# Causal attention: the mask of the exponentials as a selection on GpSimd, the maxima split there, the outputs copied by ScalarE

## The reference

```python
q = qkv[:, :, :, :Q_PER_KV].reshape(B, S, N_HEADS, HEAD_DIM)   # S = 1024, 32 heads of 16, 4 per kv head
k = qkv[:, :, :, Q_PER_KV]
v = qkv[:, :, :, Q_PER_KV + 1]
...
scores = jnp.einsum('bqhd,bkhd->bhqk', q, k) * SM_SCALE
scores = jnp.where(mask[None, None], scores, jnp.finfo(scores.dtype).min)
probs = jax.nn.softmax(scores, axis=-1)
ctx = jnp.einsum('bhqk,bkhd->bqhd', probs, v).reshape(B, S, HIDDEN)
```

## Time and profile before

| what | value |
|---|---|
| median of 3 runs | 1382.53 us (1381.4 to 1382.91) |
| the profiled execution | 1387.69 us |
| its span | 1385.9 us |
| mean granted TensorE clock | 0.904 |
| PE busy | 1159.6 us (84%) |
| DVE busy | 862.5 us (62%) |
| ACT busy | 661.4 us (48%) |
| POOL busy | 479.0 us (35%) |

### The profile page before, as it was taken

The page is one execution under the profiler, slowest core; times in us unless marked ns, Lnnn a source line. Parts: engine busy times, 40 slices in busy tenths (PEclk is TensorE's granted clock), DMA queues, the critical chain, the costliest instruction groups (busy, mean ns, idle before and its releaser), DMA issues. The chain is left out here.

```text
span 1385.9 us, 22738 instructions
## 1 busy us (share of the span) xinstructions
PE 1159.6 (84%) x6056; PEld 737.9 (53%) x6057; DVE 862.5 (62%) x1624; ACT 661.4 (48%) x1202; POOL 479.0 (35%) x434
## 2 busy tenths in 40 slices
PE   5979999995294999999997796999999908777687
PEld 4746766763172344444434574667766605455454
DVE  4857777772465888788852656777777524445542
ACT  3136666663232366666674121666666503324133
POOL 4325555553772111111113224455555442050030
PEclk9979999998597699999998897999999957978879
DMA  9256898556314430000001363779955550000001
GB/s 355 88 214 142 242 244 230 107 103 117 141 56 119 104 69 2 1 1 1 1 1 38 127 231 131 214 193 262 257 111 99 83 164 1 15 24 0 12 20 61
DMA packets 63497, 151.71 MB, mean 109 GB/s; under 512 B 12560, under 2 KB 17488, under 8 KB 58832
## 3 DMA queue, kind: packets, MB, share of 16 engines
q1 hardware_dynamic: 40224, 99.83, 21.0%
q0 software_dynamic: 22592, 50.27, 18.5%
q10 hardware_dynamic: 624, 0.92, 0.4%
HBM read 105.81 MB, written 44.97 MB: 109 GB/s over the span
## 5 line engine op out<-in xcount | busy, mean ns | idle before, releaser
L715 POOL DMA_INDIRECT moe_acc_rows<-moe_out_rows,moe_token_of x94 | 165.4, 1760 | 198.2 <-ACT moe_out_rows L790 194.9
L1721 DVE TENSOR_REDUCE causal_top<-causal_mx 128x1 f32<-128x512 f32 (+3 forms) x384 | 192.4, 551 | 52.2 <-PE causal_mx L1588 44.7
L1694 ACT ACTIVATE causal_prob<-causal_sc 128x512 f32<-128x512 f32 (+3 forms) x384 | 171.7, 489 | 94.1 <-PE causal_sc L1611 73.7
L819 DVE TENSOR_TENSOR moe_w_lo<-moe_raw,moe_w_hi 128x1024 fp32r<-128x1024 f32 x94 | 115.2, 1225 | 112.5 <-ACT moe_w_hi L778 100.5
L730 PE MATMUL moe_gu<-moe_raw,moe_xt_plain 128*128 x376 | 180.5, 603 | 2.3 <-ACT moe_w_hi L778 2.3
L1585 PE MATMUL causal_mx<-causal_ks,causal_qs 96*128 (+4 forms) x384 | 131.6, 349 | 28.0 <-DMA causal_qs<-causal_parts 15.6
L778 ACT CAST moe_w_hi<-moe_raw 128x1024 fp32r x94 | 98.2, 1045 | 94.4 <-issue 86.5
L1607 PE MATMUL causal_sc<-causal_qs,causal_ks 99*128 (+3 forms) x384 | 125.3, 334 | 1.3 <-ACT causal_prob L1694 1.0
L708 POOL DMA_INDIRECT moe_rows<-moe_xn_rows,moe_token_of x94 | 93.0, 990 | 75.9 <-DVE moe_z L828 31.5
L822 DVE TENSOR_TENSOR moe_down_lo<-moe_raw,moe_down_hi 128x1024 fp32r<-128x1024 f32 x94 | 114.5, 1219 | 0.0
L735 PE MATMUL moe_gu<-moe_w_hi,xt_hi 128*128 128x512 f32 x188 | 112.7, 599 | 0.0
(11 more groups left out here) (275 smaller groups left out, 2459.3 us busy)
## 6 DMA issues: line engine op xcount, KB each, us to landing
moe_raw<-in_w_gu SPq DMA_DIRECT2D x34, 1024.0 KB
moe_raw<-in_w_down SPq DMA_DIRECT2D x34, 512.0 KB
causal_qs<-causal_parts SPq DMA_DIRECT2D x42, 128.0 KB, 3.3
moe_acc_rows<-moe_zeros SPq DMA_DIRECT2D x2, 2304.0 KB, 15.2
moe_acc_rows<-x SPq DMA_DIRECT2D x18, 256.0 KB, 2.0
moe_xn_rows<-xn SPq DMA_DIRECT2D x2, 2048.0 KB, 10.7
x<-moe_acc_rows SPq DMA_DIRECT2D x16, 256.0 KB, 5.2
xn<-moe_acc_rows SPq DMA_DIRECT2D x16, 256.0 KB, 5.6
```

What stands on the lines that cost most here:

```text
L715: pool.indirect_dma_start(acc_rows[a], bass.IndirectOffsetOnAxis(ap=token_of[:, b - 3:b - 2].bitcast(U32), axis=0), out_rows[(b - 3) % OUT ...
L819: nc.vector.tensor_tensor(w_lo[1 - s][:, :, :], raw[:, bass.ds(at + SPLIT_AT, GU_COLS - SPLIT_AT)].rearrange("p (k n) -> p k n", k=SPLIT), ...
L1694: nc.scalar.activation(prob[u % 2][:, h, o:CH], sc[(u * QPK + h) % BANKS][:, o:CH], ACT.Exp, scale=SCALE).then_inc(exp_done, 1)
L1721: nc.vector.tensor_reduce(top[:, kc, t, h:h + 1], mx[i % BANKS][:, 0:w], AX.X, ALU.max).then_inc(mx_read, 1)
```

## The change

Five things change together, all inside this block.

1. The mask product of the exponentials (L1611) is gone, and with it the tile `mask_kq`. POOL instead sets the masked probabilities of a diagonal block to zero after ACT has written them, by one selection over four heads of 128 columns (`mask`), and the value products of these steps wait for it.
2. `split_maxima` is moved from DVE to POOL. DVE keeps the maximum over both key halves (`later_best`).
3. `read_output` is moved from DVE to ACT.
4. The turn of the second half's maxima moves from the end of step 0 to the end of step 1, with the reading of them in step 2, and the turn of the last outputs from step 1 to step 2, the division behind it from step 2 to step 3.
5. POOL's list is written out for all groups and has no loop.

```diff
 @block.gpsimd
+def split_maxima(gn, h):
+    if h:
+        pool.wait_ge(best_done, gn + 1)
+        source = best[:, :, :]
+    else:
+        pool.wait_ge(mx_read, gn * NMU + HALF0)
+        source = top[:, 0, 0:TC, :]
+    nc.gpsimd.tensor_scalar(neg[:, :, :], source, -1.0, None, ALU.mult).then_inc(neg_chain, 1)
+    ...
+def mask(g, u):
+    c, kb = STEPS[u]
+    o = kb * P - c * CH
+    pool.wait_ge(exp_done, g * (NS * QPK) + ((u + 1) * QPK + BANKS))
+    nc.gpsimd.affine_select(prob[u % 2][:, :, o:o + P], prob[u % 2][:, :, o:o + P], [[0, QPK], [1, P]],
+                            ALU.is_ge, 0.0, base=0, channel_multiplier=-1).then_inc(masked, 1)
+def group(g, first, more):
+    if not first:
+        split_maxima(g, 1)
+    values(g)
+    for u in range(NS):
+        if u in DIAGONAL:
+            mask(g, u)
+        if u == 1 and not first:
+            put_maxima(g, 1)
+        if u == C0 - 1 and more:
+            split_maxima(g + 1, 0)
+        if u == C0 + 2 and more:
+            put_maxima(g + 1, 0)
 @block.tensor
 def scores(g, u, h):
-    nc_last = nc.tensor.matmul(sc[b][:, o:CH], ..., start=True, stop=not diagonal)
-    if diagonal:
-        nc_last = nc.tensor.matmul(sc[b][:, o:o + P], ident[:, :], mask_kq[:, :], start=False, stop=True)
-    nc_last.then_inc(sc_done, 1)
+    nc.tensor.matmul(sc[b][:, o:CH], ..., start=True, stop=True).then_inc(sc_done, 1)
 def values(g, u):
-    pe.wait_ge(exp_done, g * (NS * QPK) + ((u + 1) * QPK + BANKS))
+    if u in DIAGONAL:
+        pe.wait_ge(masked, g * len(DIAGONAL) + (DIAGONAL.index(u) + 1))
+    else:
+        pe.wait_ge(exp_done, g * (NS * QPK) + ((u + 1) * QPK + BANKS))
 def group(g, first, more):
-    if u == 0 and not first:
+    if u == 1 and not first:
         pe.wait_ge(ctx_done, g * NCH)
         turn_maxima(g, 1)
-    if u == 1 and not first:
+    if u == 2 and not first:
         pe.wait_ge(neg_read, g * NCH + 2)
         turn_output(g - 1, 1)
 @block.scalar
+def read_output(g, c):
+    act.wait_ge(pv_done, g * NS + ((C0, NS)[c] + 1))
+    act.wait_ge(out_turn, g * NCH + (c + 1))
+    nc.scalar.copy(out_t[:, :], po[:, :]).then_inc(po_read, 1)
 def group(g, first, more):
-    if u == 1 and h == 0 and not first:
+    if u == 2 and h == 0 and not first:
         read_maxima(g, 1)
+    if u == 0 and not first:
+        read_output(g - 1, 1)
+    if u == C0:
+        read_output(g, 0)
 @block.vector
-def split_maxima(gn, h, units):
-def read_output(g, c):
+def later_best(gn):
+    dve.wait_ge(mx_read, gn * NMU + NMU)
+    nc.vector.tensor_tensor(best[:, :, :], top[:, 0, TC:T, :], top[:, 1, TC:T, :], ALU.max).then_inc(best_done, 1)
 def group(g, first, more):
-    if u == 2 and not first:
+    if u == 3 and not first:
         normalise(g - 1, 1)
```

More of the change, by code:

```diff
@@ L1485, in causal_attention_layer @@
             v_now = sb("v_now", [P, T, 2 * HD])
-            masks = sb("masks", [P, 2, P])
+            later = sb("later", [P, P])
             mask_qk = sb("mask_qk", [P, P], BF16)
-            mask_kq = sb("mask_kq", [P, P], BF16)
             ident = sb("ident", [P, P], BF16)
@@ L1768, in group @@
                             if more:
-                                for i in range(UPS - 1):
+                                for i in range(UPS):
                                     maximum(g + 1, UPS * u + i)
-                            if u == 0 and not first:
-                                read_output(g - 1, 1)
-                            if u == 2 and not first:
+                            if u == 3 and not first:
                                 normalise(g - 1, 1)
-                            if u == C0:
-                                read_output(g, 0)
-                            if more:
-                                maximum(g + 1, UPS * u + UPS - 1)
-                                if UPS * (u + 1) == HALF0:
-                                    split_maxima(g + 1, 0, HALF0)
                             if u == C0 + 5:
@@ L1987, in layout @@
     later = np.where(np.arange(P)[None, :] > np.arange(P)[:, None], np.float32(-1e30), np.float32(0))
-    d["masks"] = f(np.stack([later, later.T], axis=1).astype(np.float32))
+    d["later"] = f(later)
     return d
```

96 lines of the change are left out of this document (43 added, 53 removed).

## The result

The changed kernel takes **1369.76 us** (median of 4 runs, 1367.37 to 1373.52); before takes 1382.72 in the runs beside it. The ratio is **0.9909, 95% interval 0.989 to 0.9928**. A second series of the same kernel gave 1367.03 against 1380.55 (ratio 0.9908, 0.9891 to 0.9924). The forecast was 1390, slower; the change makes the kernel 13 us faster. The time lies in the range on record, the sign is wrong.

A forecast was written before the change was run, and what follows sets the result against it. PE's list was taken to bound the block. Seven middle groups at 34.95 us against 35.24 gave -2.0 us, the last group +7.7, the start +1.4: +7.1 in total, a median of about 1390 us, range 1368 to 1409.

The forecast's parts named there:

- What is A?: POOL's selection of 512 elements in diagonal steps: A, its time, taken as 1.05 us, ends 0.40 and 1.69.
- The slope of the sum: Whole kernel: total change 64A - 60.1 us, so +7.1 us at A = 1.05.
- as quick as the cast or quicker: Rival on POOL's selection: A = 0.84 gives -6 us, 1376; A = 0.40 gives about 1359; chance 0.35.
- The hand-offs: Diagonal steps, either side of POOL's selection: 0.25 us from ACT to POOL, 0.10 from POOL to PE.
- the break-even: Selection time at which the forecast's summed change for the whole kernel is zero: A = 0.94 us.
- the formula on record: Whole kernel: 64A - 60.1 us; a middle group takes 26.55 + 8A us against 35.24.
- spare time: Diagonal steps: how long A may be before PE stalls, 0.12 to 0.81 us, together 4.95 a group.
- PE's own gaps: Gaps before the value products of twelve steps, without waits for masks: 21.7 us a group.
- Beyond 0.81 each diagonal step adds all of A: Eight diagonal steps of a group: above that selection time, PE's stalls are 8A - 4.95 us.
- The stalls at u = 0 and 4 are worth about 1.3 us each: PE's waits for DVE before value products of steps 0 and 4: go when split and output copy leave DVE.
- The price of 0.06 for a mask product: Mask products on PE: 0.06 us each, 32 in a group, so 1.8 us saved.
- The step 0 selection comes 0.45 us late by this, on the path.: Group start on POOL: split (1.65 us) and value copy (0.40) precede step 0's selection, adding 0.45 us a group.

The follow-up runs named there:

- both edits: Changed kernel with the mask product on PE in the last group and the first-half output turn and division a step earlier: 1364.92 us, ratio 0.9877; repeated 1365.64 us.

## Why the prediction was wrong

**"What is A?" is the step that failed.** It took 1.05 us, "the middle between the cast and the two-input operation, since the predicate is generated and not read". Measured is 0.64, below the cast, though not below the end of 0.40. The slope of the sum at that place is what made it fatal: 64 selections by 0.41 us are 26 us, against a forecast of +7.1. The error in reasoning is to take the predicate as an addition to a pass over the data. The rows said less than I read from them: the comparison that "takes twice the cast" differs from it by its kind of operand and its output format as well, so its extra time was never shown to be the predicate's. The rival "as quick as the cast or quicker", with 0.35, was the right case; its own figure for the cast (1376) was above the result because even the cast is slower.

Here the Trainium skill was nearer than the choice made against it. GPSIMD Engine Reference, Performance versus the Vector engine, gives 768 ns for 512 elements in a tight loop without data-dependent branching, as a best case; that this is the price of a one-input operation is the prediction's reading. This trace shows less still, 640 ns for that many elements with a predicate on top; where they differ the measurement decides, and that figure is no lower bound for this instruction.

**The hand-offs were too dear.** "I take 0.25, and 0.10 from POOL to PE": the first was read from the earlier trace rows, in which POOL issues a DMA behind ACT's copy. For a compute instruction the same way costs 0.06. That is 0.24 us too much in each diagonal step, and it is a part of what set the break-even at 0.94 where 1.03 was measured. By that straight line even the forecast's own 1.05 would have given no change and not a slower kernel. With the right A the formula on record gives 64 x 0.64 - 60.1 = -19.1 us for a block that gained 15.0. It fits no better because it also counts a spare time larger than A as a gain: at A = 0.64 the steps 1, 2, 3, 5 and 9 have 0.55 us of it too much in each group, 3.85 us in seven groups. -15.3 is left. So three errors stand side by side. The hand-offs make the stalls 0.44 too large in a group (0.72 for the 0.28 that remain). PE's own gaps were taken too short: 21.7 and 0.45 for step 0, 22.15 together, where 22.9 was measured with the remaining stalls in it. These two cancel nearly; the price does not.

**"Beyond 0.81 each diagonal step adds all of A"**: this form is right only far out. From 0.64 to 0.98 a group grew by 1.0 us where eight steps grew by 2.7, from 0.98 to 1.22 by 1.1 where they grew by 1.9. With the true hand-offs the spare times are 0.36 (step 0) to 1.05, so at 0.64 only step 0 stalls, and at 0.98 still not all do.

**The savings.** "The stalls at u = 0 and 4 are worth about 1.3 us each": 3.32 to 2.06 and 3.00 to 2.09, so 1.26 and 0.91. The run without the selection gives them free of the mask products, which the forecast counted apart: 3.32 to 1.97 and 3.00 to 2.26, so 1.35, of which 0.3 was the turn that moved on, and 0.74. Both stalls were taken too large. The reason for DVE's relief holds: without the splits' move nothing is gained. Of the two, the splits are worth four times the outputs, each put back alone. The price of 0.06 for a mask product was right where PE is the bound; 32 of them are 1.9 us and not the 1.8 written, and 0.92 of it arrives. (Step 2's gap, 1.86 in the forecast's list, should be 1.81 by its own rule.)

**"The step 0 selection comes 0.45 us late by this, on the path."** POOL's timeline at a group's start shows the queue:

```profile
563.47 0.25 POOL L1558 TENSOR_SCALAR causal_neg<-causal_best 128x16 f32<-128x16 f32 x1 [0.29 <-DVE causal_best L1786]
563.79 0.20 POOL L1563 CAST causal_neg_parts<-causal_neg 128x16 bf16<-128x16 f32 x1
...
564.64 0.22 POOL L1572 TENSOR_TENSOR causal_neg_parts<-causal_left,causal_neg_parts 128x16 bf16<-128x16 f32 x1
564.81 0.40 POOL L1584 COPY causal_v_now<-causal_v_all 128x256 f32<-128x256 f32 x1
565.16 0.64 POOL L1592 TENSOR_SCALAR_AFFINE_SELECT causal_prob<-causal_prob 128x512 f32<-128x512 f32 x1
```

The split takes 1.4 us and not 1.65. The selection follows the copy with no idle time of POOL, and ends at 565.80, 0.14 before the value products. So it is late as forecast. What it costs is less than the 0.45: the kernel without any selection has a gap of 1.97 there, with four mask products in it, against 2.06, so that the wait for POOL at step 0 costs between 0.09 and 0.33, lateness and length of the selection together.

**The last group and the start.** +7.7 was forecast for the last group; it lost 3.2 there. 8 x 0.64 - 0.7 = 4.4 was the formula's figure, 1.9 less with the true hand-offs. The 1.2 us behind it no term named: the sum priced POOL as a link before the value products and left out that the block cannot end before POOL does. The later turn, put at nothing, costs 1.0 us in this group once the selection is gone from it. The first score product comes 27.14 us after the block's start (27.55 in the second profile) in place of 26.67: +0.5 to +0.9, where +1.4 stood for the slower splits.

**The checks stated.** DVE's busy time falls by (862.5 - 837.1) / 8 = 3.2 us a group, as forecast. POOL is named in PE's waits, as forecast, but for 4.5 us in all and not for 0.4 in each diagonal step. ACT's copies add 9.4 us in all, 1.2 a group where 1.3 was forecast; its whole busy time rises by less, from 661.4 to 665.5 us.

## What to carry to other kernels

When an unknown price is multiplied by 64 and the sum changes sign within its bounds, the price is the forecast: measure that one instruction first, and don't split the difference between two rows that differ from it in several things at once. Read a hand-off from a row in which the receiver starts the same kind of work; one that issues a DMA is no model for one that computes. A serial step added to every group pays in the groups where the engine it feeds has other work, and costs in the last one, where it has none: give the last group its own form. Ask too which engine now finishes the block: work moved to an engine that was long done can hold back what comes next.

## What the runs showed of the hardware

- GpSimd's selection with a generated predicate, f32 to f32 in place: 0.64 us for 128x512, 0.52 for 128x384, 0.41 for 128x256, 0.29 for 128x128. Some 0.12 us for each 128 elements over a fixed 0.18.
- ACT to POOL 0.06 us and POOL to PE 0.05 us for compute instructions, against 0.29 from ACT's copy to POOL's DMA issue. Five small dependent operations on POOL (128x16 elements) start 0.27 to 0.32 us apart, each 0.20 to 0.25 long.
- The end of a block behind POOL. Where POOL's selection is its last instruction, the next block's first DMA is issued 4.24 or 4.25 us after the selection ends, in nine of nine profiles; where POOL is long done, it is issued 0.27 or 0.28 us after DVE's last instruction, in five of five. In the first nine the transposes ahead of it take 0.63 us (two profiles) to 1.09 us, and the time is the same. The run that takes only the last group's selection away shows the cause; what fills the 4.24 us is not shown.
- TensorE's clock. The granted clock of the last 3 us of the block is 0.50 to 0.73 in the nine profiles with a selection in the last step, and 0.96 to 1.00 in the five without. PE's last wait is 0.73 to 1.66 us in the first and 0.37 in the second, but PE also has nothing to do for longer at the end of the first, so this does not show which of the two lowers it. A fall to 0.50 within a group came in the profiles with the selection twice, with the splits on DVE and with both edits; of these only the last was repeated, and there it did not come again.
